# Routing of the experts of layers 1 and 2 in two halves of eight token tiles

## The chip, the cores and the metric

The kernel runs as one program on one core of a Trainium2 chip. The metric is the device time of one execution in microseconds (us). The kernel before was timed three times: 4123.52, 4126.50 and 4128.83 us, median 4126.5 us.

## The reference, cut to what matters

Four layers are applied to x, 2048 tokens (8 x 256) of 128 features. Each has a cross attention and a feed-forward part; those of layers 0, 1 and 2 are mixtures of 16 experts. For the normalised tokens `xf` layer 1 computes (layer 2 has one matrix and relu squared in place of the gated silu, and a scale of 2.5):

```
logits = xf @ router_w.T;  scores = sigmoid(logits);  sb = scores + correction_bias
group_scores = sum of the 2 largest sb in each of 4 groups of 4 experts
masked = sb in the 2 best groups, a fill value elsewhere
topk_idx = the 4 largest of masked;  w = scores at topk_idx, divided by their sum
combine[s, e] = w where e was chosen, 0 elsewhere
h = silu(xf @ gate_w[e]) * (xf @ up_w[e])           for every expert e
routed = sum over e of (h * combine[:, e]) @ down_w[e];  plus a shared expert without weight
```

Every expert is computed for every token, and `combine` weighs its hidden values. The route of a token depends on that token alone.

## The kernel before, in words

The kernel is a chain of nine phases; `build_experts` (L2545) writes three of them: L0f, L1f and L2f. All 2048 tokens stay in SBUF as 16 tiles of 128 tokens, or 4 chunks of 512. A phase has two parts.

The opening: VectorE normalises the tiles, TensorE turns them and computes the logits into the PSUM bank `misc`, and ScalarE writes `score` (L2771). VectorE then routes in eight stages, each over all 16 tiles at once (256 elements to a partition for 16 experts): `groups`, `second`, `keep`, `masked_of`, `top`, `pick`, `weights`, `cast` (L2846 to L2917). Nearly every instruction of a stage is followed by a drain, since the next one reads its output. `cast` splits the weights into three bf16 parts (`cparts`) and signals `cp_ok`. TensorE turns `cparts` in `parts(0)` and `parts(1)`, eight 128 x 128 transposes each, one for each half of the tiles, into the PSUM banks `misc` and `yp`, and VectorE copies each into `ct` (L2921, `ct_ok`).

The loop: a step q is a pair of a chunk n and a hidden tile k, q = n x KC + k, with KC = 6 in L1f (24 steps) and KC = 9 in L2f (36 steps). In L1f k = 0 to 3 carry routed experts, in L2f k = 0 to 7; the last ones are the shared expert. Each step has these pieces:

- `products(q)` on TensorE: the first matmul (L2674, `hp`), in L1f a second one too (L2680, `up`). From q = 12 on it is three matmuls on split operands (L2657 to L2659), which need `w_lo` and `yt_lo`, made on VectorE by `low` and `turn_lo`.
- ScalarE's activation `g1` (L2758), then `gate(q)` on VectorE (L2929), which frees the PSUM bank. There are 2 such banks in L1f, 4 in L2f.
- `weigh(q)` on TensorE (L2693) spreads the weights from `ct` over the hidden rows, and `hidden(q)` on VectorE (L2936) multiplies by them, after a drain.
- `down(q)` on TensorE (L2706) accumulates into `yp`. At the end of a chunk ScalarE copies `yp` (L2764), `back` turns it into `misc` (L2653), and `finish` adds it to x (L2940).

TensorE runs A = 9 steps ahead with `products`: nine before the loop, and `products(q + 9)`, `weigh(q + 1)`, `down(q)` in iteration q. VectorE's iteration q is `gate(q + 9)`, `hidden(q + 1)`, then one `low` or `turn_lo` as long as there are any (3 iterations in L1f, 5 in L2f), then `finish` at q = KC + 1. In the opening VectorE sets one gate between two routing stages. The order on each engine is that of the code, and every engine works its queue strictly in order; nothing is planned at run time.

Of the kernel before, what the change touches and what calls it, by code (L numbers as in the profile page):

```python
# [43 lines left out]
P = 128  # L44
# [2455 lines left out]
class Experts:  # L2500
# [4 lines left out]
    def __init__(self, name, E, tiles, routed, act, fill, scale, ahead, plain):  # L2505
        self.name, self.E, self.act, self.fill, self.scale = name, E, act, fill, scale
        self.KC, self.KR, self.A, self.R, self.QF = tiles, routed, ahead, ahead + 2, plain
        self.SEL = min(E, routed)
        self.share = max(1, routed // E)
        self.pieces = [(k, min(k + 6, tiles)) for k in range(0, tiles, 6)]  # L2510
        self.NF = plain // tiles
        self.matrices = 2 if act == "silu" else 1
        self.lows = [("low", i) for i in range(len(self.pieces))] + [("turn_lo", n) for n in range(self.NF, N_CHUNK)]

# [6 lines left out]
G = 4  # L2521
# [23 lines left out]
def build_experts(nc, c, held, io, x, x_in, x_out, ahead):  # L2545
# [6 lines left out]
    with ExitStack() as ctx, ExitStack() as done:  # L2552
# [33 lines left out]
        wp = [pb(f"wp{k}", [P, CHUNK]) for k in range(2)]  # L2586
        yp, misc = pb("yp", [P, CHUNK]), pb("misc", [P, CHUNK])
        turned = [hp[NB - 1], wp[0], wp[1], yp]
        parted = [misc[:, :].bitcast(BF16), yp[:, :].bitcast(BF16)]

        x_got = [sem(f"x_got{n}") for n in range(CN)]
        c_in, sel_in, sel_ok, w1_in, wu_in, w2_in = [sem(n) for n in ("c_in", "sel_in", "sel_ok", "w1_in", "wu_in", "w2_in")]
# [36 lines left out]
        def _(pe):  # L2629
# [10 lines left out]
                mm.then_inc(logits_ok, 1)  # L2640

            def parts(pair):
                pe.wait_ge(cp_ok, 1)
                for i in range(2 * CTILES):
                    mm = pe.transpose(parted[pair][:, i * P:(i + 1) * P], cparts[:, pair * 2 * CTILES + i, :], ident_b[:, :])
                mm.then_inc(parts_ok, 1)

            def back(n):
                pe.wait_ge(ft_ok, n + 1)
                if n:  # L2650
                    pe.wait_ge(xo_ok, n)
# [43 lines left out]
            def down(q):  # L2695
                n, k = divmod(q, KC)
                if q == 0:
                    pe.wait_ge(w2_in, 16)
                    pe.wait_ge(ct_ok, 2)
                if k == 0 and n:  # L2700
                    pe.wait_ge(ft_ok, n)
                if routed(q):
                    pe.wait_ge(hid_ok, routed_to(q))
                else:
                    pe.wait_ge(gu_ok, q + 1)
                pe.matmul(yp[:, :], w2[:, k, :], hid[:, q % R, :], start=(k == 0), stop=(k == KC - 1)).then_inc(dn_ok, 1)  # L2706
# [7 lines left out]
            for q in range(A):  # L2714
                products(q)
            parts(0)
            parts(1)
            pe.wait_ge(sel_ok, 1)
            weigh(0)
            for q in range(Q):  # L2720
                if q + A < Q:
                    products(q + A)
                if q + 1 < Q:
# [82 lines left out]
        def _(dve):  # L2806
# [20 lines left out]
                dve.wait_ge(yt_hi_ok, n - c.NF + 1)  # L2827
                dve.tensor_tensor(yt_lo[:, n, :], yt[:, n, :], yt_hi[:, n, :].bitcast(F32), ALU.subtract).then_inc(yt_lo_ok, 1)

            def choose(v, limit, count, w, out, ab, eq, run):  # L2830

                wide = lambda s: s.unsqueeze(2).broadcast_to([P, TT, w])
# [4 lines left out]
                dve.tensor_reduce(cnt[:, :], ab, AX, ALU.add)  # L2837
                dve.tensor_tensor_scan(flat(run), flat((seg if w == E else seg_g)[:, :, :]), flat(eq), 0.0, ALU.mult, ALU.add)
                dve.drain()
                dve.tensor_tensor(run, run, wide(cnt[:, :]), ALU.add)  # L2840
# [6 lines left out]
            def groups():  # L2847
                dve.wait_ge(score_ok, 1)
                dve.tensor_tensor(choice[:, :, :], score[:, :, :], rb[:, :].unsqueeze(1).broadcast_to([P, TT, E]), ALU.add)
                dve.drain()  # L2850
                v = choice[:, :, :].rearrange("p t (g h k) -> p (t g) h k", g=G, h=2)
                dve.tensor_tensor(large[:, :, :], v[:, :, :, 0], v[:, :, :, 1], ALU.max)
                dve.tensor_tensor(small[:, :, :], v[:, :, :, 0], v[:, :, :, 1], ALU.min)
                dve.drain()
                dve.tensor_tensor(one[:, :], large[:, :, 0], large[:, :, 1], ALU.min)
                dve.tensor_tensor(two[:, :], small[:, :, 0], small[:, :, 1], ALU.max)
                dve.drain()
                dve.tensor_tensor(two[:, :], two[:, :], one[:, :], ALU.max)
                dve.tensor_tensor(first[:, :], large[:, :, 0], large[:, :, 1], ALU.max)
                dve.drain()  # L2860
                dve.tensor_tensor(gsum[:, :, :].rearrange("p t g -> p (t g)"), first[:, :], two[:, :], ALU.add)
                dve.drain()

            def second():
                v = gsum[:, :, :].rearrange("p t (h k) -> p t h k", h=2)
                dve.tensor_tensor(g_large[:, :, :], v[:, :, :, 0], v[:, :, :, 1], ALU.max)
                dve.tensor_tensor(g_small[:, :, :], v[:, :, :, 0], v[:, :, :, 1], ALU.min)
                dve.drain()
                dve.tensor_tensor(thr[:, :], g_large[:, :, 0], g_large[:, :, 1], ALU.min)
                dve.tensor_tensor(wsum[:, :], g_small[:, :, 0], g_small[:, :, 1], ALU.max)  # L2870
                dve.drain()
                dve.tensor_tensor(thr[:, :], thr[:, :], wsum[:, :], ALU.max)
                dve.drain()

            def keep():
                choose(gsum[:, :, :], thr[:, :], 2, G, gkeep[:, :, :], g_above[:, :, :], g_equal[:, :, :], g_run[:, :, :])

            def masked_of():
                wide = lambda s: s[:, :, :].rearrange("p t g -> p (t g)").unsqueeze(2).broadcast_to([P, TT * G, EG])
                by_group = lambda s: s[:, :, :].rearrange("p t (g k) -> p (t g) k", g=G)  # L2880
                dve.tensor_tensor(by_group(masked), by_group(choice), wide(gkeep), ALU.mult)
                dve.tensor_scalar(g_run[:, :, :], gkeep[:, :, :], -c.fill, c.fill, ALU.mult, ALU.add)
# [4 lines left out]
            def top():  # L2887
                for t in range(TT):
                    dve.max(top8[:, t, :], masked[:, t, :])
                dve.drain()  # L2890
                dve.tensor_copy(thr[:, :], top8[:, :, 3])
                dve.drain()

            def pick():
                choose(masked[:, :, :], thr[:, :], 4, E, comb[:, :, :], above[:, :, :], equal[:, :, :], run_sum[:, :, :])

            def weights():
                dve.tensor_tensor(comb[:, :, :], comb[:, :, :], score[:, :, :], ALU.mult)
                dve.drain()
                dve.tensor_reduce(wsum[:, :], comb[:, :, :], AX, ALU.add)  # L2900
                dve.drain()
                dve.tensor_scalar(wsum[:, :], wsum[:, :], 1e-20, 1.0 / c.scale, ALU.add, ALU.mult)
                dve.drain()
                dve.reciprocal(wsum[:, :], wsum[:, :])
                dve.drain()
                dve.tensor_tensor(comb[:, :, :], comb[:, :, :], wsum[:, :].unsqueeze(2).broadcast_to([P, TT, E]), ALU.mult)
                dve.drain()

            def cast():
                part = lambda k: cparts[:, :, k * E:(k + 1) * E]  # L2910
                ins = dve.tensor_copy(part(0), comb[:, :, :])
                for k in range(1, 3):
                    dve.drain()
                    dve.tensor_tensor(comb[:, :, :], comb[:, :, :], part(k - 1), ALU.subtract)
                    dve.drain()
                    ins = dve.tensor_copy(part(k), comb[:, :, :])
                ins.then_inc(cp_ok, 1)  # L2917

            def parts(pair):
# [38 lines left out]
            dve.tensor_copy(ident_b[:, :], ident[:, :])  # L2958
            norm(3)
            dve.wait_ge(zero_ok, 2)  # L2960
            groups()
            gate(0)
            second()
            gate(1)
            keep()
            gate(2)
            masked_of()
            gate(3)
            top()
            gate(4)  # L2970
            pick()
            gate(5)
            weights()
            gate(6)
            cast()
            for q in range(7, A):
                gate(q)
            parts(0)
            parts(1)
            hidden(0)  # L2980
            for q in range(Q):
                if q + A < Q:
                    gate(q + A)
# [1 line left out]
                    hidden(q + 1)  # L2985
                for kind, i in c.lows[q:q + 1]:
                    (low if kind == "low" else turn_lo)(i)
                if q % KC == 1 and q >= KC:
                    finish(q // KC - 1)
            finish(CN - 1)  # L2990
# [502 lines left out]
```

## Time and profile before

| | |
|---|---|
| median of three runs | 4126.5 us |
| the profiled execution | 4126.28 us, of which the span is 4124.4 us |
| TensorE busy | 3840.4 us (93% of the span) |
| VectorE busy | 2632.9 us (64%) |
| ScalarE busy | 2668.3 us (65%) |
| GpSimd busy | 951.4 us (23%) |
| L1f | 1080 to 1173 us of the span |
| L2f | 2725 to 2836 us of the span |

Shares are means over the whole span; L1f and L2f together are about 5% of it. In the rows below, a time is counted in us from the start of the span. PE is TensorE, PEld its weight load, DVE VectorE, ACT ScalarE, POOL GpSimd.

### The profile page before, as it was taken

Reading aid. Unit: us, or ns where it says so; the run is one execution under the profiler, and the core shown is the slowest. Engines: PE = TensorE matmul, PEld = TensorE weight load, DVE = VectorE, ACT = ScalarE, POOL = GpSimd, SP = SyncE. Lnnn points to the kernel's source line nnn. Section 1 sums busy time; section 2 is a strip of 40 time slices with the busy share of each in tenths; the row PEclk is TensorE's granted clock in tenths of the full one; section 3 lists DMA queues with packets and bytes.
Section 4 is the critical chain, followed back from the end, with each engine's and each line's share of the span. In section 5 each row is a group of like instructions: output and inputs, shape, how many; then the busy total and the mean of one; then the engine's idle time right before and its main releaser. Section 6 shows DMA issues by size and latency. Waiting matters only on the chain. (4 is left out here: it accounts for less than half of the span.)

```text
span 4124.4 us, 71234 instructions
## 1 busy us (share of the span) xinstructions
PE 3840.4 (93%) x26117; PEld 2765.1 (67%) x26117; DVE 2632.9 (64%) x6105; ACT 2668.3 (65%) x4648; POOL 951.4 (23%) x842
## 2 busy tenths in 40 slices
PE   7898899999889999999999999978999999998885
PEld 6654444445467777777777777745888888886455
DVE  7655888888565666566566566556566666654762
ACT  6523577777447676767677676734777777776752
POOL 2100000000000000000000000001777777876434
PEclk9999999999899999999999999988999999999997
DMA  2100433322100000000000000010000000000003
GB/s 79 40 1 27 75 52 51 49 42 26 47 13 1 13 1 13 1 13 13 1 13 1 13 1 1 1 45 17 9 9 9 9 9 1 1 1 14 28 5 105
DMA packets 61039, 87.82 MB, mean 21 GB/s; under 512 B 13177, under 2 KB 51467, under 8 KB 59501
## 3 DMA queue, kind: packets, MB, share of 16 engines
q1 hardware_dynamic: 54729, 73.68, 8.1%
q10 hardware_dynamic: 4464, 6.30, 0.4%
q8 instruction: 213, 3.49, 0.3%
q0 software_dynamic: 1504, 3.28, 0.2%
q14 instruction: 129, 1.06, 0.1%
HBM read 58.07 MB, written 10.08 MB: 17 GB/s over the span
## 5 line engine op out<-in xcount | busy, mean ns | idle before, releaser
L2366 POOL TENSOR_TENSOR L3a_p_lo<-L3a_wq,L3a_p_hi 128x512 fp32r<-128x512 f32 (+1 forms) x480 | 627.9, 1325 | 207.5 <-ACT L3a_p_hi L2303 196.1
L1226 DVE CUSTOM_DVE_ANT_0 L2a_sc<-L2a_score,L2a_mask_n 128x804 f32<-128x804 f32 x512 | 500.0, 991 | 211.7 <-issue 195.1
L1116 ACT ACTIVATE L2a_pt<-L2a_ring 128x512 f32<-128x512 f32 x768 | 424.7, 597 | 138.6 <-PE L2a_ring L1005 133.6
L604 ACT ACTIVATE L1a_work<-L1a_ring 128x1024 f32<-128x1024 f32 x416 | 410.7, 1028 | 148.5 <-PE L1a_ring L436 147.9
L720 DVE TENSOR_REDUCE L1a_mx<-L1a_ring 128x2 f32<-128x1024 f32 x384 | 454.4, 1221 | 37.4 <-PE L1a_ring L455 31.9
L2458 DVE TENSOR_REDUCE L3a_mx<-L3a_ring 128x1 f32<-128x402 f32 (+2 forms) x640 | 322.7, 539 | 197.4 <-PE L3a_ring L2155 188.6
L1101 ACT ACTIVATE L2a_sc<-L2a_sc,L2a_nb 128x1608 f32<-128x1608 f32 x256 | 418.4, 1636 | 34.0 <-DVE L2a_nb L1231 34.0
L1005 PE MATMUL L2a_ring<-L2a_ident,L2a_sc 128*128 128x128 f32 x3072 | 425.0, 278 | 15.6 <-ACT L2a_sc L1101 9.2
L1005 PEld LDWEIGHTS L2a_ring<-L2a_ident,L2a_sc 128*128 128x128 f32 x3072 | 342.4, 141 | 86.1 <-issue 35.9
L2302 ACT ACTIVATE L3a_wq<-L3a_ring 128x512 f32<-128x512 f32 (+1 forms) x480 | 285.1, 594 | 160.0 <-PE L3a_ring L2077 114.3
L1020 PE MATMUL L2a_res<-L2a_pt,L2a_v 128*64 128x256 f32 (+1 forms) x3328 | 373.4, 381 | 1.4 <-ACT L2a_pt L1116 1.4
L1249 DVE SCALAR_TENSOR_TENSOR L2a_k_lo<-L2a_ring,L2a_bk,L2a_k_hi 128x402 fp32r<-128x402 f32 x256 | 159.0, 634 | 259.0 <-ACT L2a_k_hi L1142 257.3
L1020 PEld LDWEIGHTS L2a_res<-L2a_pt,L2a_v 128*64 128x64 f32 (+1 forms) x3328 | 233.3, 137 | 130.8 <-issue 17.6
L2303 ACT ACTIVATE L3a_p_hi<-L3a_ring 128x512 fp32r<-128x512 f32 (+1 forms) x480 | 283.8, 591 | 0.0
L476 PE MATMUL L1a_res<-L1a_work,L1a_v 128*32 128x256 f32 (+1 forms) x3328 | 232.5, 390 | 1.1 <-ACT L1a_oraw L610 0.8
L988 PE MATMUL L2a_score<-L2a_k_hi,L2a_q_hi 64*128 64x402 f32 x1024 | 206.6, 393 | 16.6 <-DVE L2a_mx L1226 14.9
L455 PE MATMUL L1a_ring<-L1a_keys,L1a_queries 64*128 64x512 f32 (+1 forms) x1024 | 197.0, 414 | 8.4 <-DVE L1a_mx L720 7.0
L2197 PE MATMUL L3a_res<-L3a_p_hi,L3a_n_hi 128*128 128x512 f32 (+1 forms) x480 | 193.7, 404 | 4.3 <-POOL L3a_p_lo L2366 3.9
L436 PE MATMUL L1a_ring<-L1a_shifted,L1a_keys 64*128 64x512 f32 x832 | 189.8, 463 | 7.0 <-DVE L1a_mx L720 4.4
L2075 PE MATMUL L3a_ring<-L3a_q_hi,L3a_kt_hi 128*128 128x512 f32 (+1 forms) x480 | 194.2, 405 | 0.1
L2155 PE MATMUL L3a_ring<-L3a_kt_hi,L3a_q_hi 128*128 128x402 f32 (+2 forms) x640 | 187.1, 346 | 3.3 <-ACT L3a_q_hi L2288 3.1
L2077 PE MATMUL L3a_ring<-L3a_q_hi,L3a_kt_lo 128*128 128x512 f32 (+1 forms) x480 | 189.6, 395 | 0.0
(742 smaller groups left out, 8180.9 us busy)
## 6 DMA issues: line engine op xcount, KB each, us to landing
L1a_keys<-L1a_k_hi SPq DMA_DIRECT2D x224, 52.0 KB
L1a_kt<-in_ctx_t SPq DMA_DIRECT2D x8, 800.5 KB, 4.4
L2a_ct<-in_ctx_t SPq DMA_DIRECT2D x8, 800.5 KB, 4.3
L1a_keys<-L1a_k_lo SPq DMA_DIRECT2D x112, 52.0 KB
L0a_cx<-in_ctx SPq DMA_DIRECT2D x16, 320.0 KB, 4.0
L3a_cx<-in_ctx SPq DMA_DIRECT2D x16, 320.0 KB, 3.7
L2a_mask_u<-in_mask SPq DMA_DIRECT2D x16, 200.1 KB, 4.4
L3f_sent<-in_L3f_blank SPq DMA_DIRECT2D x1, 3128.0 KB
```

Source lines behind the costliest of these rows:

```text
L476: mm = pe.matmul(res[32 * r:32 * r + 32, 0:S], v[0:rows, par, jt, h * c.VE:h * c.VE + 32], probs[0:rows, (par * NU + g * CT + jt) % c.PS, ...
L604: act.activation(probs[:, (par * NU + u) % c.PS, :, :], ring[tile][:, :, :], ACT.Exp).then_inc(tile_free[tile], 1)
L720: dve.tensor_reduce(mx[:, g % 2, hf, one, :, ch], ring[tile][:, :, :], AX, ALU.max).then_inc(tile_free[tile], 1)
L1005: mm = pe.transpose(bank[:, t * P:(t + 1) * P], sc[:, r % 2, g // 3, at:at + P], ident[:, :])
L1020: mm = pe.matmul(res[e * DH:(e + 1) * DH, 0:S], v[0:rows, t, h * DH:(h + 1) * DH], pt[0:rows, t, e, :], start=(t == 0), stop=(t == CT - 1))
L1101: act.activation(sc[:, r % 2, e, :], sc[:, r % 2, e, :], ACT.Exp, bias=nb[:, r % 2, e:e + 1], scale=1.0, accum_out=sums[:, r // 2 % 2, r % ...
L1116: ins = act.activation(pt[:, t:t + 4, g // 3, q], bank[:, :].rearrange("p (t q) -> p t q", t=4), ACT.Copy)
L1226: dve.tensor_tensor_reduce(sc[:, two, e, w].rearrange("p (k j) -> p k j", k=2), score[e][:, :, 0:CH], mask_n[:, r % 2, w].rearrange("p (k ...
L2302: act.activation(probs[0:r, at % 2, 0:W], bank[0:r, 0:W], ACT.Exp)
L2303: free(act.activation(p_hi[0:r, at % PH, 0:W], bank[0:r, 0:W], ACT.Exp), "scores", k)
L2366: pool.tensor_tensor(p_lo[0:r, at % PL, 0:W], probs[0:r, at % 2, 0:W], p_hi[0:r, at % PH, 0:W].bitcast(F32), ALU.subtract).then_inc(part_o ...
L2458: free(dve.tensor_reduce(mx[:, u % 2, part, to:to + 1], bank[:, 0:valid(s, ch)], AX, ALU.max), "tops", k)
```

## The change

`spans` holds the tiles that one pass of the routing handles. For L1f and L2f it is two halves, tiles 0 to 7 and 8 to 15; for L0f, with 18 hidden tiles, it is one pass over all 16 as before. Each stage takes the span T as an argument and works on that slice of the same buffers. The stages for the first half stand in the opening, where all 16 tiles stood. Those for the second half stand in the loop, one at the end of each of VectorE's iterations 1 to 8. `parts(1)` moves from the opening into iteration 9, on TensorE to its very start, ahead of `products(18)`, and waits there for `cp_ok` = 2, that is for the second half's `cast`. It now goes into `misc`, as `yp` is in use by then.

```
+        self.spans = [slice(0, 8), slice(8, 16)] if tiles < 18 else [slice(0, 16)]
...
-        parted = [misc[:, :].bitcast(BF16), yp[:, :].bitcast(BF16)]
+        parted = [misc[:, :].bitcast(BF16), (yp if len(c.spans) == 1 else misc)[:, :].bitcast(BF16)]
...
             def parts(pair):                                   # TensorE
-                pe.wait_ge(cp_ok, 1)
+                pe.wait_ge(cp_ok, min(pair + 1, len(c.spans)))
...
             def back(n):
...
+                if n or KC > 8:
+                    pe.wait_ge(ct_ok, 2)
...
             def down(q):
...
-                    pe.wait_ge(ct_ok, 2)
+                    pe.wait_ge(ct_ok, 3 - len(c.spans))
...
             parts(0)
-            parts(1)
+            if len(c.spans) == 1:
+                parts(1)
...
             for q in range(Q):
+                if len(c.spans) == 2 and q == 9:
+                    if q > KC:
+                        pe.wait_ge(xo_ok, 1)
+                    parts(1)
                 if q + A < Q:
                     products(q + A)
...
-            groups()                                           # VectorE
+            groups(c.spans[0])
             gate(0)
-            second()
+            second(c.spans[0])
...
-            cast()
+            cast(c.spans[0])
             for q in range(7, A):
                 gate(q)
             parts(0)
-            parts(1)
+            if len(c.spans) == 1:
+                parts(1)
             hidden(0)
+            later = dict(enumerate((groups, second, keep, masked_of, top, pick, weights, cast), 1)) if len(c.spans) == 2 else {}
             for q in range(Q):
...
                 for kind, i in c.lows[q:q + 1]:
                     (low if kind == "low" else turn_lo)(i)
+                if q in later:
+                    later[q](c.spans[1])
+                if later and q == 9:
+                    parts(1)
                 if q % KC == 1 and q >= KC:
                     finish(q // KC - 1)
```

In the stages themselves only the slices change, as in

```
-                dve.tensor_tensor(comb[:, :, :], comb[:, :, :], score[:, :, :], ALU.mult)
+                dve.tensor_tensor(comb[:, T, :], comb[:, T, :], score[:, T, :], ALU.mult)
```

## Rows read from the trace of the kernel before

**Rows 1.** Windows of L1f: start:end, length, busy us (instructions) by engine, PEclk, DMA.
```profile
1097.00:1121.00 24.00, 20.62 (x53) 8.53 (x52) 19.14 (x68) 9.95 (x16) 0.00 (x0) 0.86 0.00 1
1121.00:1144.00 23.00, 22.95 (x77) 13.24 (x78) 14.79 (x22) 5.98 (x10) 0.00 (x0) 1.00 0.00 0
```

**Rows 2.** Window of L2f's loop up to its tenth step, the same columns.
```profile
2764.50:2785.50 21.00, 19.14 (x55) 8.51 (x52) 14.97 (x24) 5.38 (x9) 0.00 (x0) 0.96 0.00 1
```

**Rows 3.** Timeline of TensorE, L1f: start, duration, instruction, [idle before, releaser].
```profile
1114.17 2.08 PE L2674 MATMUL L1f_hp<-L1f_yt,L1f_w 128*128 128x512 f32 x2 [2.46 <-DVE L1f_hid L2929]
1116.04 1.75 PE L2680 MATMUL L1f_up<-L1f_yt,L1f_wu 128*128 128x512 f32 x2
1117.63 1.02 PE L2674 MATMUL L1f_hp<-L1f_yt,L1f_w 128*128 128x512 f32 x2
...
1121.05 0.38 PE L2693 MATMUL L1f_wp<-L1f_ct,L1f_sel 128*128 128x512 bf16 x1 [0.65 <-DVE L1f_ct L2921]
...
1130.33 0.39 PE L2657 MATMUL L1f_up<-L1f_yt_hi,L1f_wu_hi 128*128 128x512 f32 x1
...
1131.01 1.02 PE L2706 MATMUL L1f_yp<-L1f_hid,L1f_w 128*128 128x512 f32 x2
...
1144.04 0.80 PE L2657 MATMUL L1f_hp<-L1f_yt_hi,L1f_w_hi 128*128 128x512 f32 x1
```

**Rows 4.** Timeline of TensorE, L2f.
```profile
2762.85 1.04 PE L2645 MATMUL L2f_misc<-L2f_ident_b,L2f_cparts 128*128 128x128 bf16 x8 [7.72 <-DVE L2f_cparts L2916]
...
2764.76 0.58 PE L2693 MATMUL L2f_wp<-L2f_ct,L2f_sel 128*128 128x512 bf16 x1
...
2773.63 0.50 PE L2657 MATMUL L2f_hp<-L2f_yt_hi,L2f_w_hi 128*128 128x512 f32 x1 [1.40 <-DVE L2f_yt_lo L2828]
...
2785.16 0.79 PE L2657 MATMUL L2f_hp<-L2f_yt_hi,L2f_w_hi 128*128 128x512 f32 x1
```

**Rows 5.** Timeline of VectorE, opening of L2f: first instruction of each stage, and sizes.
```profile
2743.10 0.43 DVE L2849 TENSOR_TENSOR L2f_choice<-L2f_score,L2f_rb 128x256 f32<-128x256 f32 x1 [5.78 <-ACT L2f_score L2771]
...
2743.81 0.28 DVE L2853 TENSOR_TENSOR L2f_small<-L2f_choice 128x128 f32<-128x128 f32 x1
...
2745.33 0.69 DVE L2929 TENSOR_TENSOR L2f_hid<-L2f_hp,L2f_g 128x512 f32<-128x512 f32 x1
2745.94 0.18 DVE L2866 TENSOR_TENSOR L2f_g_large<-L2f_gsum 128x32 f32<-128x32 f32 x1
...
2747.49 0.21 DVE L2834 TENSOR_TENSOR L2f_g_above<-L2f_gsum,L2f_thr 128x64 f32<-128x64 f32 x1
...
2749.92 0.41 DVE L2881 TENSOR_TENSOR L2f_masked<-L2f_choice,L2f_gkeep 128x256 f32<-128x256 f32 x1
...
2751.62 1.31 DVE L2889 MAX8 L2f_top<-L2f_masked 128x8 f32<-128x16 f32 x16
...
2753.86 0.41 DVE L2834 TENSOR_TENSOR L2f_above<-L2f_masked,L2f_thr 128x256 f32<-128x256 f32 x1
...
2755.02 0.68 DVE L2838 TENSOR_TENSOR_SCAN L2f_run_sum<-L2f_seg,L2f_equal 128x256 f32<-128x256 f32 x1
...
2757.90 0.42 DVE L2898 TENSOR_TENSOR L2f_comb<-L2f_comb,L2f_score 128x256 f32<-128x256 f32 x1
...
2760.56 0.28 DVE L2911 CAST L2f_cparts<-L2f_comb 128x256 bf16<-128x256 f32 x1
...
2761.99 0.43 DVE L2914 TENSOR_TENSOR L2f_comb<-L2f_comb,L2f_cparts 128x256 f32<-128x256 f32 x1 [0.28 <-issue]
...
2762.70 1.28 DVE L2929 TENSOR_TENSOR L2f_hid<-L2f_hp,L2f_g 128x512 f32<-128x512 f32 x2
```

**Rows 6.** Timeline of VectorE, loop of L2f.
```profile
2768.72 0.95 DVE L2820 TENSOR_TENSOR L2f_w_lo<-L2f_w,L2f_w_hi 128x768 fp32r<-128x768 f32 x1
2769.58 0.68 DVE L2929 TENSOR_TENSOR L2f_hid<-L2f_hp,L2f_g 128x512 f32<-128x512 f32 x1
2770.36 0.69 DVE L2936 TENSOR_TENSOR L2f_hid<-L2f_wp,L2f_hid 128x512 f32<-128x512 f32 x1
```

More of the change, by code:

```diff
@@ L2828, in turn_lo, with choose @@
                 dve.tensor_tensor(yt_lo[:, n, :], yt[:, n, :], yt_hi[:, n, :].bitcast(F32), ALU.subtract).then_inc(yt_lo_ok, 1)
-            def choose(v, limit, count, w, out, ab, eq, run):
-                wide = lambda s: s.unsqueeze(2).broadcast_to([P, TT, w])
+            def choose(T, v, limit, count, w, out, ab, eq, run):
+                N = T.stop - T.start
+                wide = lambda s: s.unsqueeze(2).broadcast_to([P, N, w])
                 flat = lambda s: s.rearrange("p t e -> p (t e)")
@@ L2836, in choose @@
                 dve.drain()
-                dve.tensor_reduce(cnt[:, :], ab, AX, ALU.add)
-                dve.tensor_tensor_scan(flat(run), flat((seg if w == E else seg_g)[:, :, :]), flat(eq), 0.0, ALU.mult, ALU.add)
+                dve.tensor_reduce(cnt[:, T], ab, AX, ALU.add)
+                dve.tensor_tensor_scan(flat(run), flat((seg if w == E else seg_g)[:, T, :]), flat(eq), 0.0, ALU.mult, ALU.add)
                 dve.drain()
-                dve.tensor_tensor(run, run, wide(cnt[:, :]), ALU.add)
+                dve.tensor_tensor(run, run, wide(cnt[:, T]), ALU.add)
                 dve.drain()
@@ L2845, in choose, with groups @@
                 dve.drain()
-            def groups():
+            def groups(T):
+                N, TG = T.stop - T.start, slice(T.start * G, T.stop * G)
                 dve.wait_ge(score_ok, 1)
-                dve.tensor_tensor(choice[:, :, :], score[:, :, :], rb[:, :].unsqueeze(1).broadcast_to([P, TT, E]), ALU.add)
+                dve.tensor_tensor(choice[:, T, :], score[:, T, :], rb[:, :].unsqueeze(1).broadcast_to([P, N, E]), ALU.add)
                 dve.drain()
-                v = choice[:, :, :].rearrange("p t (g h k) -> p (t g) h k", g=G, h=2)
-                dve.tensor_tensor(large[:, :, :], v[:, :, :, 0], v[:, :, :, 1], ALU.max)
-                dve.tensor_tensor(small[:, :, :], v[:, :, :, 0], v[:, :, :, 1], ALU.min)
+                v = choice[:, T, :].rearrange("p t (g h k) -> p (t g) h k", g=G, h=2)
+                dve.tensor_tensor(large[:, TG, :], v[:, :, :, 0], v[:, :, :, 1], ALU.max)
+                dve.tensor_tensor(small[:, TG, :], v[:, :, :, 0], v[:, :, :, 1], ALU.min)
@@ L2854, in groups @@
                 dve.drain()
-                dve.tensor_tensor(one[:, :], large[:, :, 0], large[:, :, 1], ALU.min)
-                dve.tensor_tensor(two[:, :], small[:, :, 0], small[:, :, 1], ALU.max)
+                dve.tensor_tensor(one[:, TG], large[:, TG, 0], large[:, TG, 1], ALU.min)
+                dve.tensor_tensor(two[:, TG], small[:, TG, 0], small[:, TG, 1], ALU.max)
                 dve.drain()
-                dve.tensor_tensor(two[:, :], two[:, :], one[:, :], ALU.max)
-                dve.tensor_tensor(first[:, :], large[:, :, 0], large[:, :, 1], ALU.max)
+                dve.tensor_tensor(two[:, TG], two[:, TG], one[:, TG], ALU.max)
@@ L2860, in groups, with second @@
+                dve.tensor_tensor(first[:, TG], large[:, TG, 0], large[:, TG, 1], ALU.max)
                 dve.drain()
-                dve.tensor_tensor(gsum[:, :, :].rearrange("p t g -> p (t g)"), first[:, :], two[:, :], ALU.add)
+                dve.tensor_tensor(gsum[:, T, :].rearrange("p t g -> p (t g)"), first[:, TG], two[:, TG], ALU.add)
                 dve.drain()
[L2864 to L2867, printed above, removed]
+            def second(T):
+                N, TG = T.stop - T.start, slice(T.start * G, T.stop * G)
+                v = gsum[:, T, :].rearrange("p t (h k) -> p t h k", h=2)
+                dve.tensor_tensor(g_large[:, T, :], v[:, :, :, 0], v[:, :, :, 1], ALU.max)
+                dve.tensor_tensor(g_small[:, T, :], v[:, :, :, 0], v[:, :, :, 1], ALU.min)
@@ L2868, in second @@
                 dve.drain()
-                dve.tensor_tensor(thr[:, :], g_large[:, :, 0], g_large[:, :, 1], ALU.min)
-                dve.tensor_tensor(wsum[:, :], g_small[:, :, 0], g_small[:, :, 1], ALU.max)
+                dve.tensor_tensor(thr[:, T], g_large[:, T, 0], g_large[:, T, 1], ALU.min)
+                dve.tensor_tensor(wsum[:, T], g_small[:, T, 0], g_small[:, T, 1], ALU.max)
                 dve.drain()
-                dve.tensor_tensor(thr[:, :], thr[:, :], wsum[:, :], ALU.max)
+                dve.tensor_tensor(thr[:, T], thr[:, T], wsum[:, T], ALU.max)
@@ L2873, in second, with keep @@
                 dve.drain()
[L2875 to L2880, printed above, removed]
+            def keep(T):
+                N, TG = T.stop - T.start, slice(T.start * G, T.stop * G)
+                choose(T, gsum[:, T, :], thr[:, T], 2, G, gkeep[:, T, :], g_above[:, T, :], g_equal[:, T, :], g_run[:, T, :])
@@ L2881, in masked_of @@
+            def masked_of(T):
+                N, TG = T.stop - T.start, slice(T.start * G, T.stop * G)
+                wide = lambda s: s[:, T, :].rearrange("p t g -> p (t g)").unsqueeze(2).broadcast_to([P, N * G, EG])
+                by_group = lambda s: s[:, T, :].rearrange("p t (g k) -> p (t g) k", g=G)
                 dve.tensor_tensor(by_group(masked), by_group(choice), wide(gkeep), ALU.mult)
-                dve.tensor_scalar(g_run[:, :, :], gkeep[:, :, :], -c.fill, c.fill, ALU.mult, ALU.add)
+                dve.tensor_scalar(g_run[:, T, :], gkeep[:, T, :], -c.fill, c.fill, ALU.mult, ALU.add)
@@ L2885, in masked_of, with top @@
                 dve.drain()
-            def top():
-                for t in range(TT):
+            def top(T):
+                N, TG = T.stop - T.start, slice(T.start * G, T.stop * G)
+                for t in range(T.start, T.stop):
                     dve.max(top8[:, t, :], masked[:, t, :])
                 dve.drain()
-                dve.tensor_copy(thr[:, :], top8[:, :, 3])
+                dve.tensor_copy(thr[:, T], top8[:, T, 3])
                 dve.drain()
-            def pick():
-                choose(masked[:, :, :], thr[:, :], 4, E, comb[:, :, :], above[:, :, :], equal[:, :, :], run_sum[:, :, :])
@@ L2897, in weights, with pick @@
-            def weights():
-                dve.tensor_tensor(comb[:, :, :], comb[:, :, :], score[:, :, :], ALU.mult)
+            def pick(T):
+                N, TG = T.stop - T.start, slice(T.start * G, T.stop * G)
+                choose(T, masked[:, T, :], thr[:, T], 4, E, comb[:, T, :], above[:, T, :], equal[:, T, :], run_sum[:, T, :])
+            def weights(T):
+                N, TG = T.stop - T.start, slice(T.start * G, T.stop * G)
+                dve.tensor_tensor(comb[:, T, :], comb[:, T, :], score[:, T, :], ALU.mult)
@@ L2899, in weights @@
                 dve.drain()
-                dve.tensor_reduce(wsum[:, :], comb[:, :, :], AX, ALU.add)
+                dve.tensor_reduce(wsum[:, T], comb[:, T, :], AX, ALU.add)
                 dve.drain()
-                dve.tensor_scalar(wsum[:, :], wsum[:, :], 1e-20, 1.0 / c.scale, ALU.add, ALU.mult)
+                dve.tensor_scalar(wsum[:, T], wsum[:, T], 1e-20, 1.0 / c.scale, ALU.add, ALU.mult)
                 dve.drain()
-                dve.reciprocal(wsum[:, :], wsum[:, :])
+                dve.reciprocal(wsum[:, T], wsum[:, T])
@@ L2905, in weights, with cast @@
                 dve.drain()
-                dve.tensor_tensor(comb[:, :, :], comb[:, :, :], wsum[:, :].unsqueeze(2).broadcast_to([P, TT, E]), ALU.mult)
+                dve.tensor_tensor(comb[:, T, :], comb[:, T, :], wsum[:, T].unsqueeze(2).broadcast_to([P, N, E]), ALU.mult)
                 dve.drain()
-            def cast():
-                part = lambda k: cparts[:, :, k * E:(k + 1) * E]
-                ins = dve.tensor_copy(part(0), comb[:, :, :])
+            def cast(T):
+                N, TG = T.stop - T.start, slice(T.start * G, T.stop * G)
+                part = lambda k: cparts[:, T, k * E:(k + 1) * E]
+                ins = dve.tensor_copy(part(0), comb[:, T, :])
@@ L2912, in cast @@
                 for k in range(1, 3):
                     dve.drain()
-                    dve.tensor_tensor(comb[:, :, :], comb[:, :, :], part(k - 1), ALU.subtract)
+                    dve.tensor_tensor(comb[:, T, :], comb[:, T, :], part(k - 1), ALU.subtract)
                     dve.drain()
-                    ins = dve.tensor_copy(part(k), comb[:, :, :])
+                    ins = dve.tensor_copy(part(k), comb[:, T, :])
                 ins.then_inc(cp_ok, 1)
@@ L2960, in _ @@
             dve.wait_ge(zero_ok, 2)
-            groups()
+            groups(c.spans[0])
             gate(0)
-            second()
+            second(c.spans[0])
             gate(1)
-            keep()
+            keep(c.spans[0])
             gate(2)
-            masked_of()
+            masked_of(c.spans[0])
             gate(3)
-            top()
+            top(c.spans[0])
             gate(4)
-            pick()
+            pick(c.spans[0])
             gate(5)
-            weights()
+            weights(c.spans[0])
             gate(6)
-            cast()
+            cast(c.spans[0])
             for q in range(7, A):
```

## The prediction

> **What bounds the kernel now.** I read the page's busy shares first (the reader sees TensorE at 93%, so the program as a whole is TensorE's), then the windows and timelines of the two phases that the change touches, since a mean over 4124 us says nothing of 5% of it. In the opening of L1f TensorE is busy 20.62 of 24 us and VectorE 19.14; in the first nine steps of the loop TensorE has 22.95 of 23 and VectorE 14.79 [rows 1]. So the opening runs at VectorE's pace, the loop at TensorE's, with 8.2 us of idle VectorE in it. L2f has one matmul less to a step: in the same part of its loop TensorE is busy 19.14 of 21 us and VectorE 14.97 [rows 2], so neither leaves much. The timelines show what the opening costs: in L1f a gap of 2.46 us while VectorE is in `pick`, then matmul pairs of 2.08 and 1.75 us where the next takes 1.02 [rows 3]; in L2f a gap of 7.72 us before `parts(0)` [rows 4]. The loop proper starts with `weigh(0)`, at 1121.05 and 2764.76, and `products(18)`, the first piece of iteration 9, starts at 1144.04 and 2785.16 as printed. Those rows last 0.80 and 0.79 us where the same matmul lasts 0.39 in the middle of its step [rows 3, 4], so their first half is drawn over the `down` before; I count them from 1144.45 and 2785.6.
>
> **What the stages cost.** Behind each opening gate (0.61 us from start to start) stands a stage, so the starts of [rows 5] give the lengths: groups 2.23, second 0.94, keep 1.82, masked_of 1.09, top 1.63, pick 3.43, weights 2.05, cast 1.9 without its 0.28 of idle; 15.1 us together. A half: an instruction takes 0.43 us at 256 elements, 0.28 at 128, 0.21 at 64 and 0.18 at 32, the scan 0.68 at 256 (0.41 at 128 by its slope) [rows 5]. Halving so saves 0.14 on a 256-wide instruction, 0.07 on a 128-wide one, 0.04 on a 64-wide one, and 8 of 16 MAX8 at 0.08. By stage: 0.45, 0.03, 0.27, 0.29, 0.66, 1.10, 0.43, 0.50, together 3.7. A half is 11.35 us and both halves are 22.7, that is 7.6 us more VectorE work in each phase. Ends for the length of a half: 7.5 us (all cost goes with the elements) and 15.1 (none does); the five widths put it at 11.4, and another 0.5 us either way is what I trust.
>
> The Trainium skill, page "VectorE: DVE Perf Modes", section "The TRN2 errata — SBUF-src ops pay a fixed extra latency per instruction", speaks against narrow instructions; its table has 58 cycles plus one per element at 0.96 GHz, and the text under it finds some 150 cycles measured. By the table (an estimate) 256 and 128 elements would take 0.33 and 0.19 us, a half 8.9 us, and the change would cost about 8.4 us in all. The trace has 0.43 and 0.28, so it agrees with the 150 and not with the table.
>
> **The opening (gain).** L2f: VectorE is a single chain from 2743.10 to the `ct` copy, so all 3.7 us and perhaps the 0.28 of idle come off; `parts(1)` (eight transposes) and its copy leave too, but `parts(0)`'s copy still has to be waited for. `weigh(0)` comes 3.9 us earlier, at 2760.85. L1f: gates 0 and 1 wait for their matmuls, so the 0.5 us of the first two stages is lost and 3.25 counts; but the 2.46 us gap shrinks to waits of about 0.5 us each before `products(7)` and `products(8)`, TensorE keeps its full clock there, and some 0.45 us of waiting for the slow pairs goes. `weigh(0)` comes 3.7 us earlier, at 1117.35.
>
> **The loop (loss).** What matters is `parts(1)` at the head of TensorE's iteration 9: it waits for the second `cast`, which ends VectorE's iteration 8, and behind it in TensorE's queue stand `products(18)`, `down(9)` and everything later. So the question is when VectorE ends iteration 8. A gate with its `hidden` takes 0.78 + 0.61 = 1.39 us, the 0.61 as behind a gate in [rows 5], `low` of six tiles 0.86, of three half that by its width, `turn_lo` 0.61 like the other 512-wide ones [rows 5, 6].
>
> L1f, from `gate(9)` at 1119.55 (2.2 us behind `weigh(0)`): seven pairs 9.73, two gates without `hidden` 1.22, lows 2.96 (0.87 twice, 0.61 twice), `finish(0)` with its drain 0.77 (it stands ahead of `gate(17)`), the half 11.35; sum 26.0, and nothing in it waits. `cast` ends at 1145.6. TensorE, undelayed, is at iteration 9 at 1117.35 + 23.4 + 0.6 (one wait of `down(3)`) = 1141.4. It stands 4.2 us, then the transposes at half clock take 0.9, and `products(18)` starts at 1146.5 instead of 1144.45: +2.05. Its six matmuls, three in 0.68 us from start to start at full clock [rows 3], take 2.8 us for 1.4 at half of it: +1.4. L1f loses 3.5 us.
>
> L2f, from `gate(9)` at 2763.4: eight pairs 11.12, a gate 0.61, lows 3.1, no `finish` yet (it comes in iteration 10), the half 11.35, and one wait of 1.6 at `gate(12)`: the first split product waits for `yt_lo` already now (1.40 us [rows 4]), and `groups` stands just ahead of the `turn_lo` that makes it, so that gap grows to about 3.3 us. Sum 27.8, `cast` ends at 2791.2 and `products(18)` starts at 2792.2 instead of 2785.6: +6.6. Behind it: the three matmuls at half clock 0.7, `weigh` and the start of `down` 0.2, and the second `ct` copy, 0.6 us now in VectorE's chain, of which two thirds show; 1.3 together. L2f loses 7.9 us.
>
> Why the clock counts as lost: the gap of 2.46 us cost 0.95 + 0.73 = 1.7 us in the pairs behind it and the one of 7.72 left `weigh(0)` at 0.58 us for 0.38, while the gap of 1.40 did not slow its followers (0.50 is a single matmul with its start) [rows 3, 4]. The new gaps of 4.2 us (L1f), 3.3 and about 4.7 (L2f) lie above the 2.46.
>
> Everything else is nothing: L0f keeps its single pass, the added waits in `back` are for a semaphore that is long up, no DMA is moved, SP's and GpSimd's queues are not touched, and the phases behind start from x when the last `finish` is done. From `products(18)` on TensorE sets the pace as before, so the delay is carried to the end of each phase. Sum: 4126.3 (the profiled execution) + 3.5 + 7.9 = 4137.7. The median lies 0.2 above that execution, so 4138.
>
> **The rivals.**
>
> (a) The other side: the second half fits into VectorE's idle time. For it: 8.2 and 6.0 us idle in the windows [rows 1, 2]. Against: 11.35 is more than either. If the half cost nothing, TensorE would still wait for `cast` behind `hidden(9)`, 0.6 us in L1f and 1.2 in L2f, and have the 0.44 of transposes: -3.7 + 1.0 and -3.9 + 1.7, some -4.9, say -4.5, in all, 4122, faster than before. The point from which it decides is where VectorE's iteration 8 ends before TensorE's: about 6.4 us of second half in L1f and 3 in L2f; the two cancel near 5.7. So even here the gain stays within 0.2%.
>
> (b) The clock is kept through the new gaps, since the matmuls before them were dense where those before the 2.46 gap were not. Then L1f loses 2.05 - 0.45 = 1.6 to 2.2 and L2f, without both falls, 5.4 to 5.9: about +7.5, 4134 at the median.
>
> (c) A half costs more than the widths say, by fetch stalls like the 0.28 us "issue" in `cast` [rows 5] or strides of sliced tiles: each 0.6 us on the half costs 2 us in the two phases together, up to +27 for a full 15.1. At 12.5 us it is 4142.
>
> (d) The change does not do what it says: excluded by the code, as the waits name the second `cast`.
>
> **How the numbers follow.** A measurement of this kernel tells about 0.2%, 8.3 us, from no change. Chances: the forecast (+9 to +14) 0.57, (b) 0.17, (c) 0.13, (a) or anything that ends near or below the time before 0.13. Slower by over 0.2% (above 4134.8): nearly all of the first, a third of (b), all of (c): 0.72. Within 0.2%: 0.25. Faster by over 0.2%: 0.03, as the whole of the opening's gain is below it. The range: from 4130, short of (b)'s low end, to 4145, inside (c); a fifth is left out, most of it (a).
>
> **What would show it.** In the changed trace: `weigh(0)` 3.7 and 3.9 us earlier in its phase; VectorE in iterations 1 to 8 without idle time in L1f; TensorE's largest gap of each phase's loop before the transposes of `cparts` in iteration 9, released by `cast`, of 4 to 5 us, with matmuls of double length behind it; in L2f a gap of over 3 us before the first split matmul. It would be wrong if a 128-wide instruction came out well under 0.28 us, or if these gaps were not there.

## The result, and the profile after

The changed kernel takes 4142.8 us (median of 6 runs, 4139.65 to 4145.36) against 4126.3 us for the kernel before beside it (6 runs): ratio 1.0042, 95% interval 1.0032 to 1.0052, slower by 16.5 us. A second comparison of the same two gave 4140.5 against 4126.9 us, ratio 1.0040 (1.0026 to 1.0054).

I measure each phase from the start of the sigmoid that writes `score` to the start of the last `back`. L1f goes from 74.5 to 80.9 us and L2f from 92.3 to 102.2 us, 16.3 us together. The span of this one execution grew by 18.3 us; the other 2.0 lie between the two phases, in L2a. The granted clock of L2a's last 50 us is 0.75 there and 0.79 in the profile of the kernel before. A second profile of the changed kernel has 0.86 in that stretch and does not show the 2.0 us. The clock need not be all of it: a second profile of the kernel before has 0.75 there too, and L2a was only 0.9 us longer in it.

Windows of the changed kernel, L1f and then L2f, each as opening, loop up to iteration 9, and the wait; columns as in [rows 1]:

```profile
1097.00:1118.30 21.30, 18.86 (x44) 7.78 (x44) 15.43 (x59) 9.88 (x16) 0.00 (x0) 0.89 0.00 1
1118.30:1142.50 24.20, 23.34 (x77) 13.15 (x78) 19.83 (x60) 5.98 (x10) 0.00 (x0) 1.00 0.00 1
1142.50:1149.00 6.50, 1.80 (x11) 1.06 (x10) 4.07 (x12) 0.00 (x0) 0.00 (x0) 0.77 0.00 1
```

```profile
2751.00:2769.90 18.90, 11.10 (x27) 4.30 (x27) 15.36 (x59) 9.06 (x16) 0.00 (x0) 0.77 0.00 1
2769.90:2797.00 27.10, 22.34 (x51) 10.25 (x51) 19.98 (x60) 5.38 (x9) 0.00 (x0) 0.79 0.00 1
2797.00:2803.00 6.00, 1.34 (x11) 0.91 (x9) 4.21 (x13) 0.60 (x1) 0.00 (x0) 0.88 0.00 0
```

The opening of L1f is 21.3 us for the 24 of [rows 1], that of L2f 18.9 for 22 (2742.6 to 2764.76, the latter in [rows 4]). In the loop VectorE is now busy 19.83 of 24.2 us where it was 14.79 of 23 [rows 1], and a window appears that was not there: 6.5 us with 1.80 us of TensorE. Timeline of TensorE around it, L1f:

```profile
1118.32 0.38 PE L2696 MATMUL L1f_wp<-L1f_ct,L1f_sel 128*128 128x512 bf16 x1 [1.09 <-DVE L1f_ct L2938]
...
1142.15 1.13 PE L2709 MATMUL L1f_yp<-L1f_hid,L1f_w 128*128 128x512 f32 x2 [0.25 <-DVE L1f_hid L2953]
1147.97 1.01 PE L2646 MATMUL L1f_misc<-L1f_ident_b,L1f_cparts 128*128 128x128 bf16 x8 [4.70 <-DVE L1f_cparts L2933]
1148.74 0.78 PE L2660 MATMUL L1f_hp<-L1f_yt_hi,L1f_w_hi 128*128 128x512 f32 x1
1149.32 0.63 PE L2661 MATMUL L1f_hp<-L1f_yt_hi,L1f_w_lo 128*128 128x512 f32 x1
...
1153.25 0.39 PE L2661 MATMUL L1f_hp<-L1f_yt_hi,L1f_w_lo 128*128 128x512 f32 x1
```

The first row answers to the `weigh(0)` of [rows 3]: 21.4 us behind the sigmoid instead of 24.0. The 2.46 us gap and the slow pairs of [rows 3] are gone. Then 4.70 us of nothing, released by the second `cast`, and matmuls of 0.63 us, 0.43 from start to start, where the same one takes 0.39 four us later, 0.23 from start to start. The granted clock, the last column but two, is at the lower of its two levels in the 3 us behind the gap (0.50 of full speed):

```profile
1142.50:1147.90 5.40, 0.78 (x2) 0.00 (x0) 4.07 (x12) 0.00 (x0) 0.00 (x0) 0.83 0.00 2
1147.90:1150.90 3.00, 2.93 (x13) 2.57 (x14) 0.00 (x0) 0.49 (x1) 0.00 (x0) 0.50 0.00 0
1150.90:1153.90 3.00, 3.00 (x8) 1.78 (x8) 1.29 (x2) 0.11 (x1) 0.00 (x0) 0.67 0.00 0
```

In L2f the loop of TensorE has two such gaps, at the first split matmul (1.40 us in [rows 4]) and ahead of `parts(1)`. The first row is `weigh(0)`:

```profile
2769.93 0.58 PE L2696 MATMUL L2f_wp<-L2f_ct,L2f_sel 128*128 128x512 bf16 x1 [0.88 <-DVE L2f_ct L2938]
...
2781.71 0.80 PE L2660 MATMUL L2f_hp<-L2f_yt_hi,L2f_w_hi 128*128 128x512 f32 x1 [3.19 <-DVE L2f_yt_lo L2836]
...
2802.09 1.04 PE L2646 MATMUL L2f_misc<-L2f_ident_b,L2f_cparts 128*128 128x128 bf16 x8 [4.66 <-DVE L2f_cparts L2933]
```

What VectorE does ahead of the first of them, from its timeline: `groups` of the second half stands between `low` and the gate, and `turn_lo` follows behind that gate and its `hidden`.

```profile
2777.26 0.55 DVE L2828 TENSOR_TENSOR L2f_w_lo<-L2f_w,L2f_w_hi 128x384 fp32r<-128x384 f32 x1
2777.72 0.28 DVE L2859 TENSOR_TENSOR L2f_choice<-L2f_score,L2f_rb 128x128 f32<-128x128 f32 x1
2778.08 0.23 DVE L2862 TENSOR_TENSOR L2f_large<-L2f_choice 128x64 f32<-128x64 f32 x1
...
2779.26 0.19 DVE L2871 TENSOR_TENSOR L2f_gsum<-L2f_first,L2f_two 128x32 f32<-128x32 f32 x1
2779.59 0.69 DVE L2946 TENSOR_TENSOR L2f_hid<-L2f_hp,L2f_g 128x512 f32<-128x512 f32 x1
2780.37 0.69 DVE L2953 TENSOR_TENSOR L2f_hid<-L2f_wp,L2f_hid 128x512 f32<-128x512 f32 x1
2780.98 0.68 DVE L2836 TENSOR_TENSOR L2f_yt_lo<-L2f_yt,L2f_yt_hi 128x512 fp32r<-128x512 f32 x1
```

### The profile page after: what moved, and what is told of

Read it like the earlier page. It is cut to its first block and busy times, and to the rows that moved or that the text cites. A ratio compares the mean times of both kernels' runs of the same rounds, so it can differ in the third digit from the quotient of the medians.

```text
span 4142.7 us, 71381 instructions
## 1 busy us (share of the span) xinstructions
PE 3852.0 (93%) x26117; PEld 2771.2 (67%) x26117; DVE 2642.8 (64%) x6187; ACT 2668.4 (64%) x4648; POOL 951.6 (23%) x842
```

## The experiments

Two measures stand side by side. The timed median says what a kernel takes; the lengths of L1f and L2f in one profile say where. Phases without a change in them came out 0.2 to 1.2 us apart, so I read no phase difference below 1.5 us. Each ratio compares a kernel with runs of the kernel before made beside it, whose medians were 4126.3, 4126.4, 4126.9 and 4125.3 us.

| kernel | L1f us | L2f us | timed median us | ratio to before, 95% |
|---|---|---|---|---|
| before | 74.5 | 92.3 | 4126.3 | |
| before, run again | 75.1 | 92.1 | 4124.7 | 0.9997 (0.9988 to 1.0007) |
| changed | 80.9 | 102.2 | 4142.8 | 1.0042 (1.0032 to 1.0052) |
| changed, run again | 80.7 | 102.2 | 4140.5 | 1.0040 (1.0026 to 1.0054) |
| second half left out | 71.8 | 90.5 | 4119.9 | 0.9985 (0.9975 to 0.9994) |
| both halves in the opening | 80.9 | 101.6 | 4136.1 (one run) | |
| `parts(1)` late | 76.3 | 100.6 | 4128.3 | 1.0006 (0.9997 to 1.0016) |
| late, L2f's stages later too | 76.5 | 98.4 | 4127.5 | 1.0003 (0.9994 to 1.0013) |
| TensorE kept busy | 78.5 | 101.5 | 4135.3 | 1.0025 (1.0015 to 1.0035) |
| split in L1f alone | 81.0 | 92.1 | 4131.4 | 1.0012 (1.0003 to 1.0022) |
| last four stages, L1f alone | 74.2 | 93.5 | 4132.0 | 1.0015 (1.0006 to 1.0024) |
| only `parts(1)` moved | 75.7 | 93.6 | 4126.1 | 1.0001 (0.9992 to 1.0011) |

**The two kernels again.** 

> The kernel before, unchanged, as a run of its own: how far two profiled executions of one kernel differ in the stretches that no variant touches, and what the comparison makes of no change. Expected 4126 us, within 1 us of the other runs of before; L1f (from score to the last back) 74.5 us and L2f 92.3 us as in the first profile, within 0.3 us, while L0 to L1a and L2a each differ by some us.

> The changed kernel again, beside the others on one chip. Theory: L1f 81.0 and L2f 102.2 us as in its first profile, within 0.5 us, so the loss lies there and the 2.1 us that its first profile showed in L2a do not return; 4141 to 4143 us. Rival (part of the loss is in the untouched phases, by the program's length): L2a again 2 us longer than in both profiles of before.

Both phases of the changed kernel repeat within 0.3 us. Those of the kernel before repeat within 0.7 us, where 0.3 was expected; L1f's 0.7 arose in its opening. L2a's 2 us did not come back, and the changed kernel's second profiled span was 4135.2 us. Its median, 4140.5 us, is half a microsecond under the expected range. The loss lies in the two phases.

**The second half left out** (tiles 8 to 15 are not routed).

```
-                pe.wait_ge(cp_ok, min(pair + 1, len(c.spans)))
+                pe.wait_ge(cp_ok, 1)
...
-                if q in later:
-                    later[q](c.spans[1])
```

> The changed kernel without the second half's eight stages in the loop (tiles 8 to 15 are not routed, their weights are zeros); parts(1) stays in iteration 9 and waits for the first cast only. Theory (the loss is VectorE's second half): both phases keep the opening's gain of 2.7 to 3.5 us, less 0.44 us of transposes in the loop, so 4120 to 4122 us, under the kernel before. Rival (the loss comes from parts(1) in the loop, the shared bank or the longer program): over 4128 us.

4119.9 us and both phases shorter than before: the theory holds. With `parts(1)` in iteration 9, the whole gain that the change could reach is 2.7 and 1.8 us in the phases. What it loses against that comes from the second half's stages on VectorE.

**Both halves in the opening**, stage by stage, and both groups of transposes and their copies there too.

```
-            groups(c.spans[0])
+            for T in c.spans:
+                groups(T)
             gate(0)
...
```

> Both halves of each stage stand in the opening, one behind the other, parts(0) and parts(1) as before: the price of routing in two passes by itself. Theory: the two passes are 23 to 25 us for 15.1 in one, so weigh(0) comes 8 to 9 us later than before in each phase (a bit more by the clock) and nothing changes in the loop: 4142 to 4146 us. The rival that narrow instructions cost half of wide ones: weigh(0) within 1 us of before, 4127 us.

The phases grew by 6.4 and 9.3 us. In L2f that is what the theory had (8 to 9, a bit more by the clock); there `parts(0)` starts 8.2 us later in its phase. In L1f the growth is less. The single time, 4136.1, is below its range and settles little alone. The wait for `cast` ahead of `parts(0)` in L2f, 7.72 us before [rows 4], is 10.21 us here.

```profile
2774.66 1.04 PE L2646 MATMUL L2f_misc<-L2f_ident_b,L2f_cparts 128*128 128x128 bf16 x8 [10.21 <-DVE L2f_cparts L2928]
```

These phases are as long as those of the changed kernel (80.9 and 102.2). Putting the second half into the loop as the change does hid none of it in the end.

**`parts(1)` late**: in iteration 10 of L1f and 14 of L2f, on TensorE and VectorE alike.

```
+        self.turn_at = 10 if tiles == 6 else 14
-                if len(c.spans) == 2 and q == 9:
+                if len(c.spans) == 2 and q == c.turn_at:
...
-                if n or KC > 8:
+                if n:
                     pe.wait_ge(ct_ok, 2)
```

> The changed kernel with one difference: parts(1), TensorE's transposes of the second half's weights and VectorE's copy, stands in iteration 10 of L1f and 14 of L2f instead of 9; the eight stages stay where they are. Theory (the head of TensorE's queue at iteration 9 waits for the second cast): the gaps of 4.70 and 4.66 us before those transposes are gone or under 1 us; what stays is that hidden comes late, as VectorE is behind, with a wait of 1 to 3 us at down(9). By the order of the queues L1f ends about 1 us and L2f about 7 us later than before, 4134 to 4136 us. Rival (VectorE's volume alone decides, wherever parts(1) stands): no gain, 4141 to 4144 us.

In L1f the gap ahead of the transposes fell from 4.70 to 0.43 us, and 1.75 us at `down(9)` took its place:

```profile
1143.77 1.12 PE L2710 MATMUL L1f_yp<-L1f_hid,L1f_w 128*128 128x512 f32 x2 [1.75 <-DVE L1f_hid L2954]
1145.33 0.61 PE L2647 MATMUL L1f_misc<-L1f_ident_b,L1f_cparts 128*128 128x128 bf16 x8 [0.43 <-DVE L1f_cparts L2934]
```

L1f gives back 4.7 of its 6.5 us. L2f gives back 1.5 of 9.8: there the place of `parts(1)` is the smaller part, since the delayed `hidden` holds TensorE anyway. The 4.66 us gap is gone, and the longest wait for `hidden` in its place, in iteration 9, is this:

```profile
2790.64 1.10 PE L2710 MATMUL L2f_yp<-L2f_hid,L2f_w 128*128 128x512 f32 x2 [2.57 <-DVE L2f_hid L2954]
```

The timed median, 4128.3 us, is well below the expected 4134 to 4136. It came down further (14.5 us) than the two phases (6.2); that is taken up below.

**Late, and L2f's stages later too** (iterations 6 to 13, `parts(1)` in 15).

```
+        self.turn_at = 10 if tiles == 6 else 15
+        self.first_later = 1 if tiles == 6 else 6
-            later = dict(enumerate((groups, second, keep, masked_of, top, pick, weights, cast), 1)) if len(c.spans) == 2 else {}
+            later = dict(enumerate((groups, second, keep, masked_of, top, pick, weights, cast), c.first_later)) if len(c.spans) == 2 else {}
```

> The changed kernel with parts(1) in iteration 10 of L1f and 15 of L2f, and in L2f the eight stages at the ends of iterations 6 to 13 instead of 1 to 8, behind the last turn_lo. Theory (in L2f the loss is VectorE's added volume, of which the wait for yt_lo is one place): the gap before the first split matmul falls from 3.2 to 1.4 us, but hidden still comes late wherever the stages stand; L1f 76.3 us as in the variant with parts(1) late, L2f 4 to 6 us longer than before (96.5 to 98.5) instead of 9.8. Rival (only volume counts, place not at all): L2f again 100.6 us.

L2f 98.4 us, at the upper end of the theory's range, against 100.6 with the stages in 1 to 8. The gap at the first split matmul is 1.41 us again:

```profile
2770.41 0.50 PE L2662 MATMUL L2f_hp<-L2f_yt_hi,L2f_w_hi 128*128 128x512 f32 x1 [1.41 <-DVE L2f_yt_lo L2838]
```

Group of TensorE's `down` in L2f's loop, with the idle time ahead of it and its releaser:

```profile
L2711 PE MATMUL L2f_yp<-L2f_hid,L2f_w 128*128 128x512 f32 x32 | 18.3, 655 | 6.9 <-DVE L2f_hid L2955 6.9
```

In the same 45 us of the loop that wait is 1.8 us in the kernel before and 5.7 us with the stages in 1 to 8. Together with the gap at the first split matmul TensorE waits 8.3 us here, 8.9 with the stages in 1 to 8 and 3.2 before: moving the stages moved most of the waiting to another place. The rest of the 2.3 us gained fits the clock, granted 0.93 in 25 us of that loop (2767 to 2792) with the stages in 1 to 8 and 1.00 here, but the two were not taken apart.

**TensorE kept busy** by four more products into `misc`, ahead of the wait for the second `cast`.

```
+                    for _ in range(4):
+                        pe.matmul(misc[:, :], w1[:, 0, :], yt[:, 0, :], start=True, stop=True)
                     parts(1)
```

> The changed kernel with four added matmuls (128x512, about 3.4 us at full clock, results overwritten) ahead of TensorE's wait for the second cast. Theory with the clock: the gaps shrink to about 1.3 us, the granted clock stays at full behind them, products(18) and what follows run at full speed, and 1.2 to 2 us come back in each phase: 4139 to 4140.5 us. Rival (the clock behind the gap costs nothing, as the chain over VectorE sets the pace there): 4142 to 4144 us.

L1f came down by 2.5 us, L2f by 0.6, which is within the scatter. The median, 4135.3 us, is below the ranges of both theory and rival, so it decides nothing between them; the lengths and rows do. In L1f the clock stayed up (granted 1.00 from 1136 to 1148) and the split matmuls behind the transposes took 0.40 us:

```profile
1139.03 3.70 PE L2729 MATMUL L1f_misc<-L1f_yt,L1f_w 128*128 128x512 f32 x8 [1.12 <-DVEq L2961]
1142.56 0.61 PE L2646 MATMUL L1f_misc<-L1f_ident_b,L1f_cparts 128*128 128x128 bf16 x8
1142.98 0.47 PE L2660 MATMUL L1f_hp<-L1f_yt_hi,L1f_w_hi 128*128 128x512 f32 x1
...
1143.52 0.40 PE L2662 MATMUL L1f_hp<-L1f_yt_lo,L1f_w_hi 128*128 128x512 f32 x1
```

The clock share is shown for L1f, 2.5 us; for L2f it is not. There the profiles show one fall that cost nothing: behind the 3.19 us gap the granted clock is 0.50 over 6 us in the changed kernel and 0.73 here, yet `parts(1)` starts 20.4 us behind the first split matmul in both. VectorE's chain sets the pace in between.

**The split in L1f alone.**

```
-        self.spans = [slice(0, 8), slice(8, 16)] if tiles < 18 else [slice(0, 16)]
+        self.spans = [slice(0, 8), slice(8, 16)] if tiles == 6 else [slice(0, 16)]
...
```

> The changed kernel with the split for L1f alone; L2f routes in one pass. Theory (the two phases lose apart): L1f 81.0, L2f 92.3 us, about 4132.7 us.

L1f is 81.0 us and L2f, at 92.1, is at its old length: the two losses are separate. The median is 4131.4 us.

**The last four stages in halves, L1f alone.** The first four run over 16 tiles in the opening; `parts(1)` stands in iteration 10.

```
+            whole = slice(0, 16)
+            groups(whole)
...
+            later = dict(zip((3, 5, 6, 8), (top, pick, weights, cast))) if len(c.spans) == 2 else {}
...
```

> L1f alone is changed: groups, second, keep and masked_of route all 16 tiles in the opening, where gates wait anyway; top, pick, weights and cast run in halves, the second one at the ends of iterations 3, 5, 6 and 8, and parts(1) stands in iteration 10. 2.7 us come off the opening for 6.7 us put into VectorE's 8 idle us of the loop. Theory: L1f 2 us shorter than before (72.3 us), no gap above 1 us in its loop, 4124 us. Rival (the second cast is late whatever its size, since hidden stands behind each stage): L1f not shorter than before, 4126 us or more.

A miss. The loop has no gap above 0.6 us and `weigh(0)` comes 2.2 us earlier, but L1f ends at 74.2 us for 74.5 to 75.1, and the median is above the kernel before. Of the 2.2 us, 0.6 is gone by the first `back` and 1.3 more by the second. Up to there TensorE waits 0.30 us for `hidden` and 0.43 us ahead of the transposes, and the transposes take 0.42 us themselves, where the kernel before has none of the three. It is no better version, and none was found.

**Only `parts(1)` moved.** All stages run over 16 tiles in the opening; `parts(1)` stands in iteration 10 of L1f and 14 of L2f.

```
-                pe.wait_ge(cp_ok, min(pair + 1, len(c.spans)))
+                pe.wait_ge(cp_ok, 1)
...
-            cast(c.spans[0])
+            cast(whole)
...
-                if q in later:
-                    later[q](c.spans[1])
-                if later and q == 9:
+                if len(c.spans) == 2 and q == c.turn_at:
                     parts(1)
```

> One pass over all 16 tiles in the opening, and only parts(1) and its copy moved into the loop (iteration 10 of L1f, 14 of L2f), without a wait for a second cast. Theory (the split costs, the move does not): each phase within 0.7 us of before, L1f 74 to 74.8, L2f 91.7 to 92.6 us; 4125 to 4127 us. Rival (transposes and copy in the loop cost as well): each phase over 1 us longer.

Against the mean of the two profiles of the kernel before, the phases are 1.0 and 1.4 us longer; the median is the same. Neither side is clearly borne out. The move by itself costs no more than that and gains nothing; a likely reason is that TensorE's transposes stood beside VectorE's gates and copy in the opening, which no run shows apart.

## Why the prediction was right, and where its sizes were off

The forecast was 4138 us and slower; measured 4142.8 and 4140.5, inside the range of 4130 to 4145. The mechanism is there: TensorE's gaps ahead of the second `cast` of 4.70 and 4.66 us for the 4.2 and about 4.7 foreseen, the gap at the first split matmul of 3.19 for 3.3, and behind them matmuls at nearly twice the time from start to start. Of loss, 11.4 us were forecast (3.5 + 7.9) and 16.3 came. That is above the prediction's own band for its forecast (+9 to +14) and lies where it had put rival (c). Nearly every term erred to the same side, so the hit in sign and range owes hardly anything to errors that cancel. Term by term:

- The opening. `weigh(0)` came 2.6 us earlier in L1f (forecast 3.7) and 3.3 in L2f (3.9). The halved instructions took what the widths said (0.29 at 128, 0.22 at 64, 0.18 at 32 elements, the scan 0.42). What was missed is between them: a 0.42 us "issue" stall in `weights` of L1f, and a wait of 1.09 us for the `ct` copy where I had counted the savings only; TensorE used to do `parts(1)` in that time.
- The length of a half in the loop. In L1f the eight stages take 12.2 us from their first instruction to the next one behind them, for 11.35; 0.17 us of "issue" stands at the end of six of them, and 0.57 behind `finish(0)`, where the sum had none. From `gate(9)` to the end of `cast` VectorE needs 27.3 us (forecast 26.0), so `products(18)` starts 4.6 us later in its phase, for 2.05: 1.1 from the opening and 1.3 from this account for 2.4 of the 2.55. This is rival (c)'s mechanism, stalls that the widths do not show: (c) took 12.5 us for a half as its example and gave 4142.
- The clock behind the gap: L1f loses 1.9 us more from `products(18)` on (forecast 1.4). The busy TensorE experiment gave back 2.5.
- L2f: `products(18)` starts 8.9 us later (forecast 6.6), then 0.9 more (forecast 1.3). The opening accounts for 1.0 of the 2.3, up to the start of `gate(9)`; from there to the end of `cast` VectorE needs 29.2 us (forecast 27.8). The wait foreseen at `gate(12)` is there with 1.64 us; one of 0.64 us at `gate(10)`, also for ScalarE's `g`, was not in the sum.
- The attribution in L2f. The prediction laid 6.6 of 7.9 us on the wait of `parts(1)` in iteration 9. Taking that wait away gave back 1.5 us, moving the stages as well 3.8; the remaining 6.1 us are there without it. So in L2f the size of the loss was near, but the step it was laid on was not the one that holds it. The chain of VectorE's work was summed to within 1.4 us, but `down` would have waited for it anyway through `hidden`. For L1f, where 4.7 of 6.5 us went with that wait, the step stands.

Rival (a) is refuted for the amount (both halves in the opening cost as much), and its size, about -4.5 us if the half cost nothing, is what the kernel without it shows: -2.7 and -1.8. Rival (b) is refuted by the 0.63 us matmuls behind the gaps, at a granted clock of 0.50. But the clock behind the gap at L2f's first split matmul cost nothing, as said above.

An instruction of 128 elements took 0.29 us for 0.43 at 256, so some 0.15 us of each do not go with the width, and half-width instructions cost two thirds. The Trainium skill, page "VectorE: DVE Perf Modes", section "The TRN2 errata — SBUF-src ops pay a fixed extra latency per instruction", has a measured fixed term of about 150 cycles (0.16 us at its 0.96 GHz, an estimate). The trace after agrees with that and not with the 58 cycles of the page's table. The 8.4 us that the prediction gives for the table's figures does not follow from its sums: a half of 8.9 us instead of 11.35 brings the second `cast` 2.45 us earlier in each phase and leaves about 5 us of loss, an estimate. The same holds for the +27 in rival (c): at its 2 us for each 0.6 us, a half of 15.1 us gives about +24.

**Open.** The timed medians do not add up to the phases: against before, `parts(1)` late is 1.8 us slower by median and 10.1 by its phases, the last-four variant 5.1 and 0.9. Span less both phases, in twelve profiles, goes from 3949 to 3962 us, and two profiles of the changed kernel alone are 7 us apart. One place was found for the last-four variant (below); why the other programs are off in the median is open. So a difference of 2 to 5 us between two variants' medians says little on the change made.

## What to carry to other kernels

An engine's idle share in a stretch is room only if the added work fits between the operations that others wait for; add up its queue to the point where another engine waits, stalls at each stage's end included, and compare that time with the arrival of the waiting engine. A wait at the head of an in-order queue costs everything behind it, so put it as late as its consumer allows; that was worth 4.7 us in L1f, and only 1.5 in L2f, where later work of the same late engine held TensorE as well. Splitting a pass of narrow instructions in two costs half a pass again (12.2 for half of 15.1), and pays only where that extra is really hidden; no variant here gained by it.

## What the runs showed of the hardware

The granted clock of an untouched stretch changes between programs. In layer 3's self attention, the stretch of 40 us that begins 360 us behind its start ran at full clock in both profiles of the kernel before, at 0.91 in both of the changed kernel and at 0.87 in the last-four variant. Windows of that stretch, the kernel before and the last-four variant:

```profile
3941.30:3981.30 40.00, 35.26 (x333) 21.85 (x331) 29.76 (x59) 27.65 (x43) 17.04 (x14) 1.00 0.01 2
```

```profile
3941.30:3981.30 40.00, 36.02 (x297) 21.90 (x297) 27.01 (x54) 25.89 (x41) 17.01 (x14) 0.87 0.01 1
```

With the lower clock 297 matmuls fit where 333 did, and that phase was 442.0 us long for 437.1, which is 4.9 of the 5.2 us by which the last-four variant's span is longer. A lower clock in one stretch does not always lengthen the phase: with 0.91 the changed kernel took 436.8 us in both profiles; there the 36 us behind that stretch ran at 0.91 where the kernel before had 0.81. In the twelve profiles the phase takes 433.2 to 442.0 us. What makes the clock fall there in one program and not in another is open.
